# One load moved from SyncE's queue to ScalarE's, one VectorE difference and half of a Gram product moved in their queues

## The reference, cut to what matters

```
x = x + L0(gn(x))      # gn: group norm over 32 groups; L0: v + gamma * (v @ softmax(v^T v)) per image
x = x + L1(gn(x))      # h below is the x that layer 1 reads

L1(v):  v = (v - min v) / (max v - min v + eps)             # over the whole image
        m_k = box_sum(v, k) for k in 2, 4, 8, 16            # k x k window around each pixel, per channel
        l_k = log(m_k + eps)
        alpha = slope of l_k over log k                     # least squares, per pixel
        excite = sigmoid(relu(mean(alpha) @ w1 + b1) @ w2 + b2)
        sim = cosine of (l_k - mean) and (alpha log k - mean)
        return sim * sigmoid(batchnorm(alpha)) + (1 - sim) * v * excite
```

## Time and profile before

| | |
|---|---|
| median of three executions | 6843.75 us |
| the profiled execution | 6870.93 us |
| its span (first to last instruction) | 6869.2 us |
| busy: VectorE, TensorE, ScalarE, GpSimd | 80%, 74%, 70%, 26% |
| mean busy share of the 16 DMA engines in loop 3 | 71% |
| VectorE busy in loop 3 (2872 to 3568 us) | 636.2 of 696 us |

### The profile page before, as it was taken

The page is one execution under the profiler, slowest core; times in us unless marked ns, Lnnn a source line. Parts: engine busy times, 40 slices in busy tenths (PEclk is TensorE's granted clock), DMA queues, the critical chain, the costliest instruction groups (busy, mean ns, idle before and its releaser), DMA issues. The chain is left out here.

```text
span 6869.2 us, 108733 instructions
## 1 busy us (share of the span) xinstructions
PE 5112.8 (74%) x35320; PEld 4647.5 (68%) x35320; DVE 5524.0 (80%) x6453; ACT 4827.6 (70%) x5203; POOL 1757.7 (26%) x1201
## 2 busy tenths in 40 slices
PE   6968886788858888588867888588885777466643
PEld 6757776677747777477766777477774666466642
DVE  1359998689969999699986999689996999699961
ACT  0118887588848888488875888488884888588861
POOL 0022221422232222322213222322223222333310
PEclk9989998899979999799988999799997999788875
DMA  3635554577746777477755777467774666456656
GB/s 117 195 114 166 176 171 130 176 232 240 230 148 214 226 232 230 132 235 230 223 190 169 238 241 228 148 208 228 236 230 126 219 221 220 159 170 187 189 176 230
DMA packets 874516, 1344.69 MB, mean 196 GB/s; under 512 B 38705, under 2 KB 694097, under 8 KB 857937
## 3 DMA queue, kind: packets, MB, share of 16 engines
q1 hardware_dynamic: 837456, 1208.16, 51.7%
q0 software_dynamic: 36864, 134.23, 10.3%
HBM read 671.16 MB, written 536.87 MB: 176 GB/s over the span
## 5 line engine op out<-in xcount | busy, mean ns | idle before, releaser
L530 PE MATMUL even<-band,t 128*128 128x128 f32 x12288 | 1867.0, 283 | 473.9 <-ACT logs L706 293.3
L530 PEld LDWEIGHTS even<-band,t 128*128 128x128 f32 x12288 | 1625.7, 197 | 548.6 <-issue 444.4
L387 POOL TENSOR_TENSOR t<-t 128x1024 f32<-128x1024 f32 (+3 forms) x800 | 1337.3, 1683 | 1451.3 <-DVE logs L979 1408.3
L511 PE MATMUL h_ps<-mix,xt 128*128 128x256 f32 x4096 | 1054.6, 403 | 454.0 <-DVE mx L891 327.3
L511 PEld LDWEIGHTS h_ps<-mix,xt 128*128 128x128 f32 x4096 | 773.8, 199 | 603.0 <-ACT xt L693 310.7
L428 POOL DMA_DIRECT2D x1t<-logs x256 | 226.4, 884 | 2882.9 <-DVE ut L990 2815.4
L706 ACT ACTIVATE logs<-even,col 128x1024 f32<-128x1024 f32 x512 | 568.8, 1111 | 444.6 <-PE even L530 443.2
L532 PE MATMUL even<-band,t 128*128 128x128 f32 x4096 | 792.0, 275 | 0.0
L891 DVE CUSTOM_DVE_ANT_0 h_out<-h_ps,shift,mx 128x512 f32<-128x512 f32 x512 | 382.7, 748 | 488.5 <-PE h_ps L511 487.5
L488 PE MATMUL g_ps<-xa 128*128 128x257 f32 x2048 | 634.8, 391 | 152.4 <-DMA xa<-in_x_dram 152.1
L532 PEld LDWEIGHTS even<-band,t 128*128 128x128 f32 x4096 | 621.9, 192 | 0.0
(11 more groups left out here) (184 smaller groups left out, 10492.4 us busy)
## 6 DMA issues: line engine op xcount, KB each, us to landing
xa<-in_x_dram SPq DMA_DIRECT2D x256, 512.0 KB, 4.5
xb<-in_x_dram SPq DMA_DIRECT2D x256, 512.0 KB, 5.5
h_scratch<-h_out SPq DMA_DIRECT2D x128, 1024.0 KB, 7.7
hr<-h_scratch SPq DMA_DIRECT2D x256, 512.0 KB, 6.0
q_scratch<-ut SPq DMA_DIRECT2D x256, 512.0 KB, 2.7
x1t<-logs POOLq DMA_DIRECT2D x256, 512.0 KB, 5.1
p_scratch<-x1t SPq DMA_DIRECT2D x256, 512.0 KB, 3.1
pd<-p_scratch SPq DMA_DIRECT2D x256, 512.0 KB, 6.1
```

The lines of the kernel that those rows point to most:

```text
L387: ins = g.tensor_tensor(dst[:, hf, d:d + n, :], src[:, hf, d:d + n, :], src[:, hf, e:e + n, :], ALU.add)
L511: ins = t.matmul(h_ps[:, r * C:(r + 1) * C], xt[:, q % 2, jh, r, :], mix[:, jh, :], start=(jh == 0), stop=(jh == 1))
L530: ins = t.matmul(o, src[:, hf, at, :], band[:, which, :], start=True, stop=(which < 3))
```

## The change

- SyncE no longer issues the hr loads inside the loops. ScalarE does, directly behind the second pass of `offset_and_x1`, without a wait of its own. The four hr loads at the start of each loop (32 in all of 256) stay on SyncE. The loads aren't issued in the last pair except in its first half chunk, so ScalarE's loop is now 6 turns long and its last pair is written out once more.
- VectorE takes the third difference (`high_contrast`) ahead of the second eviction.
- TensorE takes the second half of the Gram product behind the first turn_back, ahead of the second mix_x.

```diff
 sync, half_chunk:
-                if Cs and not (began and hf == 0) and not (last and (k, hf) != (0, 0)):
-                    sp.wait_ge(odd_filled, 2 * u)
-                    apart()
-                    if hf == 1:
-                        load_rows(nC + 2, 1 - k, 0)
-                    else:
-                        load_rows(nC + 1, k, 1)
 tensor, half_chunk:
                     box(u, k, hf, 1)
-                if A:
-                    gram_rows(n, hf, 1)
                 if Cs:
                     box(u, k, hf, 3)
...
                 if Ds:
                     turn_back(2 * nd + hf, hf, 0)
+                if A:
+                    gram_rows(n, hf, 1)
                 if Bs:
                     mix_x(nb, 2 * hf + 1)
 scalar:
+            def load_rows(n, half, hf):
+                a.dma_start(hr[:, hf, half * ROWS:(half + 1) * ROWS, :],
+                            h_dram[n].rearrange("w (r c) -> w r c", c=C)[:, :, hf * CH:(hf + 1) * CH]
+                            ).then_inc(h_loaded[hf][half], 16)
 scalar, half_chunk:
                 if tail:
                     offset_and_x1(u - 1, nC if hf == 1 else nC - 1, 1 - hf)
+                if tail and not (last and (k, hf) != (0, 0)):
+                    if hf == 1:
+                        load_rows(nC + 2, 1 - k, 0)
+                    else:
+                        load_rows(nC + 1, k, 1)
                 if Cs:
                     log(u, hf, 0)
 vector, half_chunk:
                 if Cs:
                     low_contrasts(u, hf)
+                    high_contrast(u, hf)
                 if Bs:
                     copy_h(nb, k, 2 * hf + 1, first, None)
-                if Cs:
-                    high_contrast(u, hf)
```

More of the change, by code:

```diff
@@ L761, in copy_out, with half_chunk @@
                              o_ps[:, :].rearrange("p (r c) -> p r c", c=CH), ACT.Copy).then_inc(o_copied, 1)
-            def half_chunk(s, i, k, hf, A, Bs, Cs, Ds, first):
+            def load_rows(n, half, hf):
+                a.dma_start(hr[:, hf, half * ROWS:(half + 1) * ROWS, :],
+                            h_dram[n].rearrange("w (r c) -> w r c", c=C)[:, :, hf * CH:(hf + 1) * CH]
+                            ).then_inc(h_loaded[hf][half], 16)
+            def half_chunk(s, i, k, hf, A, Bs, Cs, Ds, first, last):
                 n = 16 * s + 2 * i + k
@@ L799, in turn, with pair @@
             def turn(s, A, Bs, Cs, Ds):
-                def pair(i, first):
+                def pair(i, first, last):
                     for k in range(2):
                         for hf in range(2):
[L803 to L806, removed]
+                            half_chunk(s, i, k, hf, A, Bs, Cs, Ds, first and k == 0 and hf == 0, last)
+                pair(0, True, False)
+                with own.loop(1, PAIRS - 1, ACT_PAIR if Cs else 0) as i:
+                    pair(i, False, False)
+                pair(PAIRS - 1, False, True)
                 if Cs:
```

## The result

The changed kernel took 6692.55 us (median of four executions, 6680.36 to 6695.8) against 6843.64 before: a ratio of 0.977 (95% interval 0.975 to 0.979), 151 us less. In a second comparison the ratio was 0.976 (0.974 to 0.977). The forecast was 6631, the range 6590 to 6745. The direction and the range held; about 60 us of the forecast gain did not come in the first measurement.

The account below looks back on a forecast made before the run. VectorE was taken to bound the loops, its hr and h_ps waits being the removable time. Terms 108 + 88 + 10 + 8 = 214 us gave 6657 us profiled, 6631 us as median; range 6590 to 6745.

Parts of the forecast that it names:

- What bounds: Inside the loops VectorE is the bound; shortening its waits for hr and for h_ps shortens the loop.
- The hr load: Loads moved to ScalarE's queue land 5.3 to 6.0 us after issue, before VectorE is ready: 108 of 127.4 us saved.
- the two ends: Load on ScalarE's queue: either shares engines with the stores, saving 108 us, or gets turns as they drain, saving nothing.
- The statement that the cause was SyncE's queue: VectorE's hr wait, 127.4 us, arises because SyncE issues the load behind two stores of 1 MB each.
- ScalarE's price: Issue on ScalarE delays the log by 0.6 us, absorbed by its 0.80 us wait for VectorE's slopes: 0, at most 269 us.
- The sign that I had named against it: New ScalarE gaps of over a microsecond behind L714 would show that the issue's cost was wrong.
- The rival in which ScalarE is blocked: Issuing hr loads holds ScalarE up, delaying box sum 3 and evictions; at 2.0 us per issue 6900 us; chance 0.06.
- The third difference: Ahead of the second eviction, 1.22 us of VectorE's work fills its wait for the second mix_x: 88 of 92 us.
- The Gram rows: Moving half the Gram product starts box sum 3 earlier: 10 us at loop 0's first evictions, 8 us at loop starts.
- The start of the loops: VectorE's wait for the first mix_x shortens by 1.3 us in the six loops with a Gram product: 8 us.
- The first, no earlier landing: The hr load gets turns only as the stores drain; other terms stay: 106 us gained, 6738 us; chance 0.15.
- The move to the first eviction: In five loops VectorE waits 22 us each at first evictions, as loop 0 does: 6741 us; chance 0.10.

Follow-up runs that it names:

- xa_first: Kernel of sp_first with SyncE's loads of xa and xb issued ahead of the store of p instead of behind it; 0.970 of the kernel before.
- sp_first_only: Kernel before, with only the hr load moved ahead of the two stores on SyncE; 0.981 of the kernel before, 130 us less.
- no_hr: Changed kernel without its first part: hr load stays on SyncE behind the stores; 0.985 of the kernel before, 98 us less.
- sp_first: Changed kernel with the hr load back on SyncE, ahead of the two stores; 6644.6 us, 0.969 of the kernel before.

## Why the prediction was right or wrong

**What bounds.** Right. VectorE's waits fell by 188 us and the span by 175. Hiding more of TensorE's (xa_first) brought nothing.

**The hr load, 108 us.** Wrong in size, and it is the step that failed: "it takes the least landing of 3.9 us and once more its own transfer". The trace gives 67 us. I had the two ends right, but chose the near one by treating the sharing as one of bytes, half the engines each. It goes by packets: beside packets of 8 KB the load got 12% of the engines instead of half, and landed 11.2 us after its issue instead of 5.3 to 6.0. Its own queue meant a tenth of the bytes (0.07 of 0.79 MB) as long as the large packets ran. And its first packet came 3.6 us after the issue, a delay for which the forecast had no term. What saved half of the term was something else that I had bounded from the wrong side: the issue is not 0 to 1.1 us later than on SyncE but 2 us earlier relative to VectorE's need. Two things are in that, as far as the traces show: ScalarE's queue doesn't wait for its engine's passes, and on SyncE the load stood behind the stores' own waits. The statement that the cause was SyncE's queue held: a place ahead of the stores (sp_first_only) takes away the whole 127 us.

**ScalarE's price, 0 us.** Right, but not for the reason given. I had the issue slip the log by 0.6 us and VectorE's slopes absorb it. In the rows shown the issue runs beside the passes and nothing slips. The sign that I had named against it did appear: gaps of over a microsecond behind the second pass, 61 instead of 29. But every one of them ends with TensorE's box sum 0, and with the load on SyncE there are 50 (no_hr) and 81 (sp_first), so they are not the issue's. The rival in which ScalarE is blocked would have needed 1.75 us per issue; the longest of 224 took 0.67.

**The third difference, 88 us.** Right: the waits of second evictions went from 90.7 to 0.2 us in the changed kernel, and to 5.5 with this edit alone. The slow second mix_x, which was to go with it, went nearly: 6 of 224 took over 2.8 us instead of 39, the longest 3.53.

**The Gram rows, 10 and 8 us.** The first evictions gave 18 us instead of 10 (35.6 to 17.4 over all loops). Its larger effect was written down only as a help to the third difference: filling TensorE's gap keeps its clock up and takes 45 us from the second evictions by itself. In the sum this doesn't count twice, since the third difference covers the same waits (85 and 74 us alone, 116 together).

**The start of the loops.** Expected 8 us. From the last contrasts of a loop to the first of the next, the seven gaps changed by about 3 us in sum, and the first loop began 3 us earlier; 6 of the 8 us, too little to be told apart. VectorE's waits for the first mix_x of the seven loops fell by 9 us in sum.

**The sum.** 108 - 67 = 41 us missing at hr, about 15 more than forecast at the evictions (121 against 106, the starts among them). 188 instead of 214 us of waits, of which the span shows 175; where the other 13 went was not traced. The rest of the way to 151 is the comparison itself: the profiled execution before stood 27 us above its median, the one after 3 us, and the second measurement of both gave 168.

**Rivals.** The first, no earlier landing, was half right: 60 of 127 us stayed. The move to the first eviction did not come: 0.8 to 1.3 us per loop in loops 1 to 5, and 4.8 in loop 6, leaving out each loop's first.

## What to carry to other kernels

A load that is late behind stores wants a place ahead of them, if what it waits for is ready by then, and not necessarily a queue of its own: with two queues the engines alternated packet for packet in these runs, and the one with the small packets got little. Before moving a DMA to another queue, compare its packet size with that of what runs beside it. And where an engine waits for a bank that another has just filled, put independent work of its own there on both sides: one engine is busy instead of waiting, the other keeps its clock.

## What the runs showed of the hardware

- Two hardware queues were served one packet for one: 140 to 143, 475 to 473 and 491 to 482 packets in windows of 2 us, with packets of 512 bytes against 8 KB and 1 KB. In the first of these windows each of the 129 data packets of one queue was followed within 6 ns by one of the other. While the load's packets began it was 112 to 346 and 179 to 445.
- A 512 KB load on ScalarE's queue had its first packet 3.6 us after its issue in half chunks with stores, and 2.3 in the others (medians of 70 each), while SyncE's queue filled the engines (104.3% from 3053 to 3055 us).
- A DMA on ScalarE's queue was issued 1.6 us before the start of a pass that stands ahead of it in the program, in 0.55 us (the median of 224 issues), and the engine's passes beside it showed no gap.
- After an idle stretch of 3.68 us TensorE ran eight matmuls in 3.75 us, at the lower level of its clock (granted 0.50); after one of 2.09 us, with Gram rows ahead of it, in 1.97 (granted 1.00).
